# Spare products on TensorE between the first projections and the first scores of a gated attention and mixture-of-experts block

## What is computed

```python
# x: 16 batches x 512 rows x 256; ctx: 16 x 64 x 128; 16 heads of 16 columns
h  = layernorm(x)
a  = causal_attention(h @ Wq, h @ Wk, h @ Wv) + attention(h @ Wcq, ctx @ Wck, ctx @ Wcv)
x  = x + tanh(g_xattn) * (a @ Wp + bp)
f  = layernorm(x)
w  = top-2 of softmax(f @ router_w + router_bias), 16 experts, the last one is the identity
r  = sum over chosen experts: w_e * (silu(f @ gate_e) * (f @ up_e)) @ down_e
s  = (silu(causal_conv3(f)) * (f @ shared_up)) @ shared_down
out = x + tanh(g_ffn) * (s + r)
```

## Time and profile before

| | |
|---|---|
| median of three runs | 1547.11 us (1543.27 to 1548.83) |
| profiled execution, its own time | not listed apart from the three runs |
| its span, first to last instruction | 1501.5 us |
| TensorE busy | 1407.1 us (94%) |
| VectorE busy | 1195.5 us (80%) |
| ScalarE, GpSimd busy | 871.1 us (58%), 902.8 us (60%) |
| mean granted clock of TensorE | 0.989 |

### The profile page before, as it was taken

How to read it: one execution, slowest core, us unless ns; L and a number is a source line. 1 busy time by engine, 2 the same in 40 slices (tenths; PEclk the granted TensorE clock), 3 DMA queues, 4 the chain that set the end, 5 groups by cost and what they waited for, 6 DMA issues and landing times.

```text
span 1501.5 us, 36135 instructions
## 1 busy us (share of the span) xinstructions
PE 1407.1 (94%) x11224; PEld 947.2 (63%) x11288; DVE 1195.5 (80%) x3122; ACT 871.1 (58%) x1811; POOL 902.8 (60%) x1643
## 2 busy tenths in 40 slices
PE   3899999999999999999999999999988999999997
PEld 3456565565555665566555655655544899999775
DVE  6878798888888888888888878888855676787686
ACT  3466666666666666766666666666560566666210
POOL 4245466666747575666657475666655566776772
PEclk8999999999999999999999999999998999999999
DMA  6844455545464556455464546455573477565795
GB/s 173 203 134 131 136 153 160 147 139 178 129 169 136 154 140 178 130 150 177 118 181 130 154 139 170 142 156 153 152 227 137 138 228 231 172 178 175 251 342 168
DMA packets 184124, 250.01 MB, mean 167 GB/s; under 512 B 32025, under 2 KB 134561, under 8 KB 183937
## 3 DMA queue, kind: packets, MB, share of 16 engines
q1 hardware_dynamic: 149680, 185.60, 44.2%
q0 software_dynamic: 13008, 36.65, 6.8%
q10 hardware_dynamic: 21248, 25.46, 5.2%
HBM read 150.06 MB, written 95.97 MB: 164 GB/s over the span
## 4 chain that ended last, share of the span: by engine, by line
PE 64%; DVE 23%; issue 4%; ACT 4%; DMA 3%; POOL 1%; SPq 0%; DVEq 0%; POOLq 0%
DVE nmax L1261 10%; PE pv_self L1504 9%; PE vector_bank L2000 8%; PE scalar_bank L1440 8%; PE vector_bank L1477 6%; PE vector_bank L1550 3%; PE vector_bank L1414 3%; DVE q L1201 3%; PE vector_bank L1474 2%; PE scalar_bank L1427 2%; PE scalar_bank L1428 2%; PE scalar_bank L1430 2%; PE pv_cross L1486 2%; PE scalar_bank L1987 2%; PE pv_cross L2008 2%
## 5 line engine op out<-in xcount | busy, mean ns | idle before, releaser
L1261 DVE TENSOR_REDUCE nmax<-vector_bank 128x1 f32<-128x384 f32 (+4 forms) x832 | 509.1, 639 | 49.1 <-PE vector_bank L1477 45.1
L901 ACT ACTIVATE pt<-scalar_bank 128x512 f32<-128x512 f32 x640 | 361.1, 602 | 213.6 <-PE scalar_bank L1440 208.8
L731 POOL TENSOR_SCALAR_AFFINE_SELECT pt<-pt 128x256 f32<-128x256 f32 (+1 forms) x640 | 221.3, 360 | 205.9 <-ACT pt L901 184.0
L1440 PE MATMUL scalar_bank<-stack 99*64 99x512 bf16 (+4 forms) x1280 | 284.0, 319 | 1.8 <-ACT ct L901 0.6
L1477 PE MATMUL vector_bank<-stack 96*128 96x128 bf16 (+3 forms) x1024 | 244.2, 301 | 17.0 <-DMA stack<-qk_scratch 11.5
L1829 POOL DMA_INDIRECT rows<-pt x143 | 139.2, 973 | 80.4 <-issue 63.7
L1504 PE MATMUL pv_self<-pt,vst 128*32 128x512 f32 (+3 forms) x2048 | 161.0, 438 | 0.1
L690 POOL DMA_INDIRECT rows<-xn,slot x128 | 132.8, 1037 | 44.2 <-issue 26.3
L1474 PEld LDWEIGHTS vector_bank<-tri,ident_b 128*128 128x128 bf16 x704 | 66.8, 97 | 138.1 <-DVE nmax L1261 62.9
L1474 PE MATMUL vector_bank<-tri,ident_b 128*128 128x128 bf16 (+1 forms) x640 | 150.6, 235 | 2.5 <-DVE nmax L1261 0.8
L2000 PE MATMUL vector_bank<-pt 128*128 128x128 f32 x1144 | 151.3, 275 | 0.0
(11 more groups left out here) (320 smaller groups left out, 2834.4 us busy)
## 6 DMA issues: line engine op xcount, KB each, us to landing
qk_scratch<-parts SPq DMA_DIRECT2D x31, 1200.0 KB, 4.6
stack<-qk_scratch SPq DMA_DIRECT2D x120, 192.0 KB, 3.0
pt<-rows SPq DMA_DIRECT2D x143, 132.0 KB
stack<-qk_scratch SPq DMA_DIRECT2D x248, 72.0 KB, 2.6
stack<-qk_scratch SPq DMA_DIRECT2D x124, 128.0 KB, 3.1
stack<-qk_scratch SPq DMA_DIRECT2D x240, 36.0 KB, 2.2
pt<-rows SPq DMA_DIRECT2D x8, 1024.0 KB, 8.8
stack<-rows SPq DMA_DIRECT2D x8, 1024.0 KB, 11.4
```

The costliest lines, as they stand in the source:

```text
L731: pool.affine_select(out=v, in_=v, compare_op=ALU.is_ge, fill=0.0, base=0, pattern=pat, channel_multiplier=-1).then_inc(masked, 1)
L901: act.activation(dst, bank(kind, b, ("st", c, k))[:, :], ACT.Exp, scale=SCALE).then_inc(scalar_drained, 1)
L1261: dve.tensor_reduce(dst, src, axis=AX, op=ALU.max, negate=True).then_inc(vector_drained, 1)
L1440: return pe.matmul(out, stack[c][0:rows, head, key0:key0 + nk], stack[c][0:rows, head, q0:q0 + nq], start=True, stop=True, **kw)
```

## The change

A new function `busy_rows` issues products on TensorE whose results nobody reads, and the prologue calls it between the last projection of c = 1 and `rest_placed()`. It issues, in this order: for 512, 256 and 128 columns 16 pairs each of fp32r products, one half of a pair with partitions 0 to 63 into `pv_self`, the other with partitions 64 to 127 into `pv_cross`; 16 fp32r products of 128 partitions and 128 columns, in turn into the two banks; and for 512 and 128 columns 16 pairs each of bf16 products of `ident_b` with `tri`. None of them waits for a semaphore or increments one.

```diff
@@ -1354,6 +1354,22 @@
                 pe.wait_ge(route_pool, 6)
                 pe.wait_ge(router_padded, 1)
 
+            def busy_rows():
+
+                for columns in (512, 256, 128):
+                    for n in range(16):
+                        for low, ps in ((0, pv_self), (64, pv_cross)):
+                            pe.matmul(ps[:, 0:columns], wq["q"][low:low + 64, n % KC, n // 2 % KC, :], xnT[low:low + 64, n % KC, 0:columns],
+                                      start=True, stop=True)
+                for n in range(16):
+                    pe.matmul((pv_self, pv_cross)[n % 2][:, 0:P], wq["q"][:, n % KC, n // 2 % KC, :], xnT[:, n % KC, 0:P], start=True,
+                              stop=True)
+                for columns in (512, P):
+                    for n in range(16):
+                        for low, ps in ((0, pv_self), (64, pv_cross)):
+                            pe.matmul(ps[:, 0:columns], ident_b[low:low + 64, :], tri[low:low + 64, 0:columns // P, :], start=True,
+                                      stop=True)
+
             def claim_s(kind, b, name):
 
                 n = SU.upto(kind, b, name) - RING
@@ -1660,6 +1676,7 @@
                             for k in (2 * i, 2 * i + 1):
                                 max_unit(kind, b, 1 - c, k)
                     if kind == "pro" and c == 1:
+                        busy_rows()
                         rest_placed()
                         for k in range(SM_PRE):
                             max_unit(kind, b, 0, k)
```

## The result

The changed kernel takes 1553.38 us (median of 20 runs, 1546.61 to 1556.42), the kernel before 1548.19 us (20 runs, 1536.34 to 1553.21): a ratio of **1.0034**, 95% interval 1.002 to 1.0049. The forecast of 1549.1 us was 4.3 us low. It was a delay of 2.0 us set on a median of three runs, and the delay measured is 5.2; the direction, "no change of 0.5%" and the range held.

What follows compares the result with a forecast made beforehand. VectorE's reductions set the pace behind a TensorE gap ended by a DMA at 36.17 us; added products of 13.9 us end at 38.4, 2.0 us late: 1547.1 + 2.0 = 1549.1 us, range 1543.5 to 1562.

Steps and rivals of the forecast that it cites:

- The price of the added products: Time of the six added groups on TensorE, in order of issue: 13.9 us, from 24.5 to 38.4 us.
- C and D: Added fp32r groups of 128 columns, 16 pairs and 16 whole products: 0.11 us apiece, bound by the load, 1.8 us each group.
- E: Added group of 16 bf16 pairs of 512 columns: about 0.23 us a pair, 3.7 us.
- Overlap by rows: Claim that the two halves of an added pair run beside each other, as column tiles do, costing one product.
- The first rival: Pairs run one after the other: added products take 25.3 us, first reduction 13.4 us late, 1560.5 us; chance 0.24.
- the second rival: Products overlap but four-byte weight loads don't: 17.2 us of added products, 5.3 us late, 1552.4 us; chance 0.20.
- The first reduction: VectorE's first reduction behind the gap: start at 38.83 instead of 36.84 us, 2.0 us late, nothing downstream absorbing it.
- All that a warm TensorE can give back is 0.24 us: From first score product to first reduction: 0.67 us cold, 0.43 us warm; VectorE sets the pace behind it.
- granted clock 1.00 from 20 to 50 us: Sign that the forecast is right: TensorE's clock stays full through the filled gap and the first maxima.
- The fourth rival: Added products don't hold the clock if half-filled rows don't count: 11.9 us late, 1559 us; chance 0.05.
- Pass-through: Claim that the 2 us delay at the first reduction stays the same at 60 us and at the end.
- The sum against the median: Left 45.6 us between the 1501.5 us span and the 1547.1 us median as they are; added 2.0 us to the median.

Runs made afterwards that it cites:

- run 5: The changed kernel with both products of each pair on partitions 0 to 63, so they can't overlap; ratio 1.018 to the kernel before.
- the trimmed kernel: The changed kernel without its 16 fp32r pairs and 16 bf16 pairs of 128 columns; ratios 1.0005 and 1.0001 to the kernel before.

## Why the prediction was right or wrong

**The price of the added products was right to 0.1 us.** Forecast 3.7 + 1.9 + 1.8 + 1.8 + 3.7 + 1.0 = 13.9 us; measured 3.76 + 1.91 + 1.86 + 1.93 + 3.46 + 0.99 = 13.9. The bounds of C and D (128 columns of fp32r at 0.055 or 0.23 us) both fell: products and pairs follow each other by 0.11 us inside the groups, the cadence of the load, as the nearest row had it. E was 0.24 too dear, since I took a finish time for a cadence (0.216 us a pair).

**Overlap by rows: right.** The halves of a pair start less than 0.03 us apart. The first rival is out for the changed kernel; run 5 shows the halves in turn at 0.23 us when they share partitions.

**Loads side by side: right, against the second rival.** A half load is 0.18 us long, a whole one 0.19, and both halves' loads start at 24.70. The rule of the Trainium skill (TensorE: Matmul & The Clock Gate, LDWEIGHTS) holds, the trace agrees: the length doesn't go by the rows. But it says nothing against two at once. The Trainium skill, TensorEngine Tiling (Array Packing), Tiling Modes, Key Properties, says that different tiles can load and multiply in parallel; here the trace agrees too. The measured time, 5.2 us over before, happens to be what the second rival gave (5.3), for another reason; that is coincidence.

**The first reduction: 2.0 us forecast, 2.4 measured, 2.6 on average.** Of the 0.4 us that were missing, 0.2 is the start: the added products begin at 24.70 us and not at 24.5, behind the second of the two products that the row at 24.20 merges. The other 0.23 us are in the step that took the way from the first product to the reduction. The first product of a maximum is the mask (L1474, 512 columns), and its 64 records are missing in the first profile of before: there the page counts 640 products of L1474 beside 704 loads. In the third profile it is there, at 35.90 us:

```profile
35.90 0.59 PE L1474 MATMUL vector_bank<-tri,ident_b 128*128 128x512 bf16 x1 [10.92 <-DMA stack<-qk_scratch]
36.28 0.63 PE L1477 MATMUL vector_bank<-stack 96*128 96x128 bf16 x4
```

So TensorE had to be free some 0.4 us sooner than 36.17 (36.28 - 35.90, the mask at half clock), and the mask's warm 0.23 us belongs to the way from the last spare product to the first reduction (38.61 to 39.27 us, 0.66 and not 0.43). The two counts on the page would have told.

**"All that a warm TensorE can give back is 0.24 us": right as a bound for a gain, wrong as the only effect of the clock.** I had looked at what the cold stretch costs and had put what the clock does behind it at nothing. This is the term that was missing: 1.2 to 2.3 us in each of the four profiled executions of the changed kernel. Why it falls there is open. It is not warmth alone: the trimmed kernel comes in warm and kept its clock in both profiles, and two variants that came in cold lost it. All eight executions with a late first reduction lost it. The recorded sign "granted clock 1.00 from 20 to 50 us" failed accordingly: 0.83 from 40 to 50.

**The fourth rival had a real mechanism, in the wrong kernel.** With half-filled rows of 128 columns the clock fell, at 32.3 us; pairs, which fill all rows, kept it at 1.00 up to the maxima.

**Pass-through: right up to 1044 us.** By run 5 it is 1:1: 25.9 us and a fall's 2.3 make 28.2, and 28.0 is left at 1044 us. The sign that I had named for being wrong altogether, that the delay at the first reduction isn't the delay at the end, did come up for the changed kernel: 2.4 to 3.4 us at the first reduction and 5.2 in the runs. The delay wasn't absorbed, it grew, by the falls and by the 1.4 us behind 1044 us that stay open.

**The sum against the median: wrong in its reading.** The 45.6 us "around the span" don't exist; it is 2.1 to 2.4 us, and the profile was of an execution some 44 us faster than the median. It did no harm because only differences in the prologue were used. I should have asked whether such a rest is plausible.

**Range.** 1543.5 to 1562 held 1553.4; what stretched it to the slow side were rivals that the runs ruled out for this kernel, while part of the loss that came was one it didn't name. What is measured is 0.34%, of which the working accounts for the overrun, about half; that the total still lies well inside the range is owed to the width of the range.

## What to carry to other kernels

Work that fills a wait is free only up to the moment at which the wait would have ended, and that moment moves from one execution to the next (the first reduction of before came at 36.3 to 37.3 us); leave a margin. Warming TensorE for a stage that VectorE paces gives back only the latency of its first product, 0.24 us here. A change that starts such a stage late can cost more than the delay, if the clock falls behind it as it did here; look at the granted clock behind the changed place, in several executions. When a span and the median of the runs are 3% apart, profile again before any long stage is compared.

## What the runs showed of the hardware

- Two products on different halves of the rows, into different banks, cost what one whole product costs: 0.23 us for 512 columns of fp32r with its load, 0.216 us in bf16, 0.12 and 0.11 us for 256 and 128 columns of fp32r, 0.056 us for 128 of bf16. Their weight loads overlap too.
- fp32r products of 128 columns follow each other by 0.11 us, like their loads; 128 columns aren't dearer than the load.
- The clock fell on a TensorE that didn't pause: amid products that filled half the rows with 128 columns each, 0.11 us apart, the granted clock went from 2.4 to 1.2 GHz at 32.3 us in one run and at 39.3 us in another. With 512 and 256 columns in half the rows it held in one execution, and with fp32r products of 128 columns in all rows, in pairs or whole, in all that had them warm.
- The nine falls behind the first reduction lasted 3.4 to 6.8 us and cost 1.2 to 2.3 us each. In the 8 us ahead of seven of them no pause between products was over 0.3 us; the other two (57.0 and 58.3 us) came in a pause of 1.4 us.
- The expert stage with the rest up to the end, from 1145 us on, took 357 us in one execution and 393 to 405 us in the thirteen others, at a clock of 1.00 from 1160 to 1400 us in both profiles shown.
